# The head of a spectral image tower: one PSUM bank and then three for ScalarE, and the second product an image later

## The reference, cut to what matters

```python
for sw, cw, cb in ((sw0, cw0, cb0), (sw1, cw1, cb1), (sw2, cw2, cb2), (sw3, cw3, cb3)):
    x1 = _spectral_conv(x, sw)
    x2 = jnp.einsum('bchw,oc->bohw', x, cw) + cb[None, :, None, None]
    x = _gelu(x1 + x2)
x = jnp.transpose(x, (0, 2, 3, 1))
x = _gelu(x @ fc1_w + fc1_b)          # 32 channels -> 64 hidden
return (x @ fc2_w + fc2_b)[..., 0]    # 64 hidden -> 1
```

```python
h = _L0_tok_ref(...)
h = h + _L0_attn_ref(_layernorm(h, axis=-1), ...)
h = h + _L0_ffn_ref(_layernorm(h, axis=-1), ...)
```

## Time and profile before

| what | value |
|---|---|
| median of three timed executions | 1736.97 us |
| these three | 1724.95, 1737.28, 1736.97 us |
| the profiled execution's own time | 1721.6 us |
| its span, first to last instruction | 1719.6 us |
| the head in it, first product of image 0 to the barrier | 1261.1 to 1420.5 us |

### The profile page before, as it was taken

The page is one execution under the profiler, slowest core; times in us unless marked ns, Lnnn a source line. Parts: engine busy times, 40 slices in busy tenths (PEclk is TensorE's granted clock), DMA queues, the critical chain, the costliest instruction groups (busy, mean ns, idle before and its releaser), DMA issues. The chain is left out here.

```text
span 1719.6 us, 47103 instructions
## 1 busy us (share of the span) xinstructions
PE 1587.7 (92%) x21500; PEld 900.3 (52%) x21500; DVE 1201.3 (70%) x1409; ACT 585.9 (34%) x788; POOL 140.4 (8%) x64
## 2 busy tenths in 40 slices
PE   8799999997999999889999997999988889989996
PEld 3455555555555555555555555777731118833332
DVE  3498989876989898688989886555500008946777
ACT  2432222223222222233222222444478885500000
POOL 1000000000000000000000000000000000067764
PEclk9999999999999999999999999999999999999998
DMA  5133232243665656455555551899986642085551
GB/s 200 66 124 130 118 136 111 118 185 107 246 233 210 239 206 244 148 188 214 228 221 222 225 227 67 297 355 359 362 324 234 228 141 90 16 192 148 141 141 37
DMA packets 64980, 321.48 MB, mean 187 GB/s; under 512 B 18896, under 2 KB 20880, under 8 KB 30992
## 3 DMA queue, kind: packets, MB, share of 16 engines
q1 hardware_dynamic: 39984, 182.97, 31.9%
q10 hardware_dynamic: 24800, 135.51, 19.4%
HBM read 181.08 MB, written 137.36 MB: 185 GB/s over the span
## 5 line engine op out<-in xcount | busy, mean ns | idle before, releaser
L820 ACT ACTIVATE act_c<-slots,conv_b 128x512 f32<-128x512 f32 x512 | 352.3, 688 | 735.4 <-PE slots L540 735.4
L540 PEld LDWEIGHTS slots<-inv_w,inv_out 128*128 128x128 f32 x4096 | 499.4, 196 | 188.2 <-issue 179.0
L540 PE MATMUL slots<-inv_w,inv_out 128*128 128x128 f32 x4096 | 541.7, 287 | 3.2 <-DVE inv_out L715 3.2
L715 DVE STREAM_TRANSPOSE inv_out<-slots 128x1024 f32<-128x1024 f32 x256 | 304.5, 1228 | 99.1 <-PE slots L505 99.1
L691 DVE STREAM_TRANSPOSE turned_h<-slots 128x1024 f32<-128x1024 f32 x200 | 237.9, 1228 | 31.3 <-PE slots L439 30.9
L680 DVE STREAM_TRANSPOSE turned_w<-act_c 128x1024 f32<-128x1024 f32 x192 | 225.3, 1216 | 1.1 <-ACT act_c L820 1.1
L439 PE MATMUL slots<-turned_w,fwd_w 32*64 32x512 f32 x3200 | 198.7, 603 | 3.8 <-DMA turned_w<-in_x_turned_dram 2.6
L1644 POOL TENSOR_TENSOR modes<-at_turned,modes 128x1024 f32<-128x1024 f32 x14 | 34.9, 2498 | 1524.5 <-DMA at_turned<-level_scratch 1509.4
L831 ACT ACTIVATE inv_out<-slots,b 128x1024 f32<-128x1024 f32 x128 | 135.7, 1111 | 21.2 <-PE slots L638 21.2
L451 PE MATMUL slots<-turned_h,fwd_h 64*64 64x320 f32 x1600 | 137.2, 454 | 1.3 <-DVE turned_h L691 1.3
L697 DVE STREAM_TRANSPOSE modes<-slots 128x640 f32<-128x640 f32 x96 | 80.9, 845 | 79.9 <-PE slots L451 79.9
(11 more groups left out here) (151 smaller groups left out, 1021.5 us busy)
## 6 DMA issues: line engine op xcount, KB each, us to landing
act_scratch<-act_c ACTq DMA_DIRECT2D x128, 1024.0 KB, 5.1
act_c<-act_scratch SPq DMA_DIRECT2D x128, 1024.0 KB, 5.2
at_turned<-level_scratch SPq DMA_DIRECT2D x36, 256.0 KB, 4.1
at_ret_t<-level_scratch SPq DMA_DIRECT2D x34, 256.0 KB, 4.0
mode_w<-in_sw_dram SPq DMA_DIRECT2D x20, 320.0 KB, 3.3
xin<-in_x_dram SPq DMA_DIRECT2D x4, 1024.0 KB, 8.4
at_straight<-level_scratch SPq DMA_DIRECT2D x16, 256.0 KB, 4.1
at_crossed<-level_scratch SPq DMA_DIRECT2D x16, 256.0 KB, 4.0
```

The lines of the kernel that those rows point to most:

```text
L540: mm = nc.tensor.matmul(banks[:, p, at:at + 128], inv_out[:, t % 2, i, p, :, :, r].rearrange("p b o -> p (b o)"), inv_w[:, i, :], start=Fa ...
L715: nc.vector.transpose(dst, src).then_inc(inv_turned, 1)
L820: nc.scalar.activation(act_c[:, t % RING, :, p, :], banks[:, p, :].rearrange("p (i m) -> p i m", i=2), ACT.Gelu, bias=conv_b[:, l:l + 1]). ...
```

## The change

ACT now takes the shared bank by itself (128 x 512 numbers) and then the image's three own banks in one instruction (128 x 1536). PE does the second product of image n - 2, not n - 1, after the first product of n, and the loop has one turn more. There are three `unit` buffers; the third lies over `xin[:, 0]`, which the first layer no longer needs. ACT's wait on the second product goes from the image two before to the one three before. `head_bank` stays. Lines move down by three in PE's head, and by four in ACT's.

```diff
         inv_out = sb("inv_out", [128, 2, 2, 4, 4, CH, 2])
-        unit = inv_out[:].rearrange("p k i a b o r -> p k (i a b o r)").rearrange(
-            "p k (a n) -> p k a n", a=4)
+        unit = [inv_out[:, b].rearrange("p i a b o r -> p (i a b o r)").rearrange("p (a n) -> p a n", a=4)
+                for b in range(2)]
+        unit += [flat(xin[:, 0]).rearrange("p (a n) -> p a n", a=4)]
...
-        def first_parts(n):
-
-            return (0, 2) if n % 2 else (2, 0)
+        def unit_parts(n):
+
+            shared = slice(0, 1) if n % 2 else slice(3, 4)
+            own = slice(1, 4) if n % 2 else slice(0, 3)
+            return shared, own
...
-            for n in range(IMAGES + 1):
+            for n in range(IMAGES + 2):
                 if n < IMAGES:
...
-                if n > 0:
-                    i = (n - 1) % GROUP
-                    pe.wait_ge(unit_set, 2 * n)
-                    if i == 0 and n > 1:
-                        pe.wait_ge(front.rows_set, (n - 1) // GROUP)
+                if n > 1:
+                    done = n - 2
+                    i = done % GROUP
+                    pe.wait_ge(unit_set, 2 * done + 2)
+                    if i == 0 and done > 0:
+                        pe.wait_ge(front.rows_set, done // GROUP)
                     for a in range(4):
                         mm = nc.tensor.matmul(banks[a * 32:(a + 1) * 32, 7, :], w2_at[:, i * 32:i * 32 + 32],
-                                              unit[:, (n - 1) % 2, a, :], start=(i == 0), stop=(i == GROUP - 1),
+                                              unit[done % 3][:, a, :], start=(i == 0), stop=(i == GROUP - 1),
                                               skip_group_check=True)
...
                 act.wait_ge(fc1_done, n + 1)
-                if n >= 2:
-                    act.wait_ge(fc2_done, n - 1)
-                for a in first_parts(n):
-                    at = head_bank(n, a)
-                    nc.scalar.activation(unit[:, n % 2, a:a + 2, :], banks[:, at:at + 2, :],
-                                         ACT.Gelu, bias=b1[:, 0:1]).then_inc(unit_set, 1)
+                if n >= 3:
+                    act.wait_ge(fc2_done, n - 2)
+                for part in unit_parts(n):
+                    at = slice(head_bank(n, part.start), head_bank(n, part.stop))
+                    nc.scalar.activation(unit[n % 3][:, part, :], banks[:, at, :], ACT.Gelu,
+                                         bias=b1[:, 0:1]).then_inc(unit_set, 1)
```

## The result

| what | before | changed |
|---|---|---|
| median of the timed executions | 1733.53 us (6) | 1713.62 us (6) |
| lowest and highest | 1724.95, 1737.28 us | 1700.66, 1719.70 us |
| the profiled execution's own time | 1721.6 us | 1719.7 us |
| first product of image 0 to the barrier, in that execution | 159.3 us | 138.7 us |

The ratio is 0.9889, 95% interval 0.9857 to 0.992: the medians differ by 19.9 us where 20.5 were forecast, and the changed kernel's is 1713.6 us where 1716.5 were. The interval leaves room for 14 to 25 us, and it is clear of no change. Two later sets of timed executions of the same change gave 0.9873 (0.983 to 0.9916) and 0.9886 (0.9852 to 0.9921).

What follows compares the result with a forecast made beforehand. The head was taken as bound by PE and ACT waiting for each other, 2.429 us an image; 2.07 after the change saves 0.36 over 57 intervals, 20.5 us, so 1736.97 becomes 1716.5 us, range 1699 to 1725.

Steps and rivals of the forecast that it cites:

- The ring through the shared bank: Head: ACT's first instruction, handover, PE's first product, handover; before the change 2.38 us, or 2.48 for even images.
- PE alone, 2.04 to 2.08: Head: PE's own need per image, 1.05 us after a first product plus 0.99 after a second, or 2.08 us.
- The unseen sequence: Head, PE: a first product right behind a second product without a wait, shown by no row; taken as 0.99 us.
- PE turns slowly: Rival, head: second to first product takes 1.17 us, an image 2.22, gain 12 us, total 1725; chance 0.14.
- ACT alone, 2.02: Head: ACT's own need per image, 0.688 + 1.534 us less two overlaps of 0.10; 2.12 without overlap between images.
- The ring, 1.96 and 2.06: Head after the split: 0.69 + 0.05 + 1.12 + 0.10 = 1.96 us, 2.06 for even images, mean 2.01.
- The sum for an image: Head: the largest limit at each step gives 2.04 to 2.12 us; 2.07 taken, a gain of 0.36 an image.
- Which images: Head: images 0 to 5 give nothing as image 6 waits for a load; 57 intervals of 0.36 gain 20.5 us.
- The later second product, the third buffer, the groups, SP, traffic: Head: side effects expected to be hidden; copy fits by 0.1 us, worst load costs 0.9 up to three times.
- slower by SP's queue: Rival, head's groups: row stores and token loads delay later loads, three times; at 13 us each 1756 us; chance 0.03.
- the loads becoming the ring: Rival, head: each pair waits for a load, so the gain shrinks, at the old 4.86 us a pair to nothing; chance 0.07.
- The whole: Whole kernel: median 1736.97 - 20.5 = 1716.5 us, 1.2% faster.

Runs made afterwards that it cites:

- only the ring left: Changed kernel with the second product cut to 256 of 512 columns and ACT's second instruction to two of three banks; 2.002 us an image.
- ACT alone: Changed kernel with both of PE's products cut to 256 of 512 columns, ACT's work whole; 2.008 us an image.
- the later second product alone: Changed kernel with ACT taking two banks and two banks as before, later second product and third buffer kept; 2.429 us an image, ratio to before 1.0008.
- four loads ahead: Changed kernel with pairs 0 to 3 of the head loaded during the last layer, run twice; 2.049 us an image, ratios to before 0.9902 and 0.9922.
- three banks first: Changed kernel with ACT's order turned round, three banks including the shared one, then one bank; 2.856 us an image, 1761.03 us in all.

## Why the prediction was right, point by point

**The bound.** The ring through the shared bank: shown by three sizes of ACT's first instruction, which follow first instruction + 1.27 or 1.37 us (two banks 2.38 and 2.48, three banks 2.81 and 2.91, and one bank 1.95 and 2.05 with only the ring left).

**PE alone, 2.04 to 2.08.** Measured 2.040. The unseen sequence takes 0.99 to 1.00 us, like the row with the idle matmuls. The rival "PE turns slowly" (1.17 us, 2.22 in all) is out. The Trainium skill, page "TensorEngine Tiling (Array Packing)", section "Key Properties", says that a change of tiling mode drains TensorE; at both changes of an image (32 x 64 and 128 x 32) the step takes the 1.05 and 0.99 us that the rows of before had, not more.

**ACT alone, 2.02.** Measured 2.008. The instruction on three banks, costed at 1.534 us from two rows, takes 1.533.

**The ring, 1.96 and 2.06.** Measured 1.95 and 2.05.

**The sum for an image.** I took 2.07 of 2.04 to 2.12; it is 2.049. The term was 0.02 us too large: 57 intervals give 21.7 us, not 20.5.

**Which images.** This is the step that failed: "images 0 to 5 give nothing", and with it the sign "image 6 still started by a landing at about 15 us after image 0". In none of the changed kernel's three profiles did a load start image 6, which came 16.07, 12.26 and 12.99 us after image 0. In the first, the six intervals cost 1.0 us more than before: the load of pair 2 held image 4 for 2.11 us, and two products ran at about half the clock (1.97 and 1.86 us for 1.12 and 1.06), which I had not priced. In the other two they gave 2.8 and 2.1 us. The gain of the head is 20.7, 24.5 and 23.8 us against the one profile of before. I had taken one execution's landing of one load (its 0.84 us wait) for a fixed thing. What loads and the clock added to the loop's own period in these images was 0.5 us before and 3.8, 0 and 0.7 us in the changed kernel. It isn't only the faster loop that makes it vary: the later second product alone, with the old period, lost 2.2 us there with no load named as a wait, while the granted clock was 0.50 for 6.8 us from 2.7 us after image 0 on.

**The later second product, the third buffer, the groups, SP, traffic.** All hidden as argued: the end of the head 3.39 us for 3.40, the copy fits by 0.17 us for 0.1, stores at 1.84 us for 1.9, the load behind the tokens at 10.4 for 11.3. The DMA share from image 6 to the last second product was 0.68, 0.70 and 0.70 in the three profiles, under the 0.74 of the sum and above the 0.63 of before. No load held PE after image 6 in any profile of the changed kernel. The rival "slower by SP's queue" is out, and that of the loads becoming the ring holds for the first six images alone.

**The whole.** 19.9 us of 20.5, and 21.0 and 22.9 in the two later sets (medians). Two parts of this are luck. The sum left out 1.2 us in images 6 to 63 and counted nothing for images 0 to 5, which gave between -1.0 and 2.8; it came close because the two are small. And the forecast of 1716.5 us stood on the median of three executions of before, 1736.97, which became 1733.53 with three more (3.4 us less); that, and not the gain, put the measured median 2.9 us under the forecast. The heads' 20.7 to 24.5 us lie inside the interval of 14 to 25 us, so a difference from the medians' 19.9 is not shown.

## What to carry to other kernels

Where two engines hand a bank to and fro, write the ring down (instruction on what is shared + handover + product + handover) beside what each engine needs alone; only the shared bank's part belongs into the first instruction, and the rest of the work may be as long as the engine's own sum allows. The cut pays fully only if nothing else in the partner's in-order queue waits for the long instruction: here a lag of one more image and one more buffer were worth 0.14 us of 0.38, and without the cut nothing. Before a transfer is moved into another stage, look at what that stage moves already in its undisturbed executions, and add the transfer's own time to it: here 11.6 us for a gain of at most 3.8.

## What the runs showed of the hardware that I had not expected

- **A recorded ACT duration can be 0.35 us too long.** With PE cut down, ACT's waits are met early, and its 1536 numbers are recorded as 1.893 us and its 512 as 1.036 (1.533 and 0.687 in the changed kernel), 2.93 together, while an image takes 2.008. Starts, not durations, give the throughput. One kernel shows it.
- **A second semaphore on a first product costs 0.10 us** in this ring, although its wait was met long before: 2.05 us with it, 1.95 to 1.96 without. On an instruction that has slack it costs nothing.
- **The clock after the barrier differs between executions of like kernels.** In the first 60 us after the barrier the granted clock was 1.00 in nine profiles, which took 298 to 300 us from the barrier to the end. It was at 0.50 for 6.8 us in two (the later second product alone, and ACT alone), which took 300.4 and 300.5. It was at 0.50 for 13.7 us, from some 25 us after the barrier on, in three: the changed kernel's third, the first with four loads ahead, and three banks first. These took 303.3, 305.1 and 304.4. The changed kernel's other two profiles have the same instructions and no such stretch. The cause is open.
- **The last layer takes 215 to 230 us** from its first mixing matmul to the head, in fourteen profiles, with the same instructions in all but the two with four loads ahead. That is a spread of 15 us, three quarters of what the change is worth, and nothing but the median evens it out. In the twelve without the extra loads its length goes with PE's idle time ahead of loads of activations: none in the five profiles of 215 to 216 us, 1.0 and 1.1 us in the two of 218, 1.7 and 3.5 in those of 220.2 and 219.3, and 9.7, 10.0 and 12.4 in those of 226.1, 228.9 and 230.4. In the three long ones the transfers were not at their fastest: 313 to 319 GB/s from 1160 to 1260 us, where the five without a wait moved 350 to 359. Why the loads come late in some executions was not tried.
